# Four of six gated products of a chunk to ScalarE and GpSimd instead of three, with new order tables

## The reference

```
x = x + 0.5 * ffn(ln(x))
x = x + attn(ln(x))        # a selective scan (state space) block
x = x + 0.5 * ffn(ln(x))

ffn(v):  h = silu(v @ wg.T / 127) * (v @ wu.T / 127)      # 768 hidden channels
         return h @ wd.T / 127
attn(v): u  = silu(causal convolution of v with 4 taps)
         dt = softplus(v @ Wp[:64].T @ W_dt.T + b_dt)
         for each of 16 states s:  A~ = exp(dt * A_s),  B~ = (A~ - 1) / A_s
                                   h_s[t] = A~[t-1] * h_s[t-1] + B~[t-1] * u[t-1]
         y  = sum over s of C_s * h_s
         return ((y + u * D) * silu(v @ W_z.T)) @ W_out.T
```

## Time and profile before

| | |
|---|---|
| three runs | 2330.20, 2331.53, 2331.81 us (median 2331.53) |
| the profiled execution | 2330.55 us, of which the span is 2328.8 us |
| busy | PE 2129.7 us (91%), DVE 2169.8 (93%), ACT 1977.5 (85%), POOL 1817.2 (78%) |
| table loads on ScalarE | 271 in the loop and 1 ahead of it |
| first scan of row 0 starts | 88.42 us |
| first scan of row 1, row 14, row 15 starts | 236.26, 2017.50, 2150.78 us |
| last scan ends | 2278.05 us |
| granted TensorE clock | 0.977 over the span |

### The profile page before, as it was taken

How to read it: one execution, slowest core, us unless ns; L and a number is a source line. 1 busy time by engine, 2 the same in 40 slices (tenths; PEclk the granted TensorE clock), 3 DMA queues, 4 the chain that set the end, 5 groups by cost and what they waited for, 6 DMA issues and landing times. The chain is left out here.

```text
span 2328.8 us, 27774 instructions
## 1 busy us (share of the span) xinstructions
PE 2129.7 (91%) x8708; PEld 1280.0 (55%) x8708; DVE 2169.8 (93%) x2361; ACT 1977.5 (85%) x2876; POOL 1817.2 (78%) x1382
## 2 busy tenths in 40 slices
PE   7986999999999999999999999999999999999578
PEld 3452556556565555656555564655556465555246
DVE  2499999999999999999999999999999999999993
ACT  5988898898989889898988989888898988988772
POOL 2477788888888888888888888888887888888663
PEclk9997999999999999999999999999999999999779
DMA  2122344434344443443344334434434344333221
GB/s 89 38 74 72 131 139 138 143 128 150 133 141 140 137 143 131 140 142 145 136 137 143 129 136 143 148 136 137 145 128 145 137 137 145 137 127 124 73 66 38
DMA packets 112024, 291.15 MB, mean 125 GB/s; under 512 B 11201, under 2 KB 45314, under 8 KB 111874
## 3 DMA queue, kind: packets, MB, share of 16 engines
q1 hardware_dynamic: 111874, 289.35, 36.4%
HBM read 271.49 MB, written 17.83 MB: 124 GB/s over the span
## 5 line engine op out<-in xcount | busy, mean ns | idle before, releaser
L1118 POOL TENSOR_TENSOR acc<-acc,ring 128x1024 f32<-128x1024 f32 x512 | 1022.8, 1998 | 141.6 <-DVE ring L1314 131.0
L1278 DVE TENSOR_TENSOR_SCAN g_bank<-du_bank,ring 128x1024 f32<-128x1024 f32 (+1 forms) x512 | 1097.7, 2149 | 9.1 <-ACT du_bank L1021 6.6
L791 PE MATMUL work<-wd_t,hid 128*128 128x256 f32 x3072 | 681.5, 381 | 6.0 <-DVE hid L1231 5.1
L1314 DVE SCALAR_TENSOR_TENSOR ring<-g_bank,inv_a,ring 128x1024 f32<-128x1024 f32 (+1 forms) x576 | 662.3, 1155 | 9.9 <-POOL acc L1118 1.8
L791 PEld LDWEIGHTS work<-wd_t,hid 128*128 128x128 f32 x3072 | 584.1, 191 | 107.0 <-issue 14.8
L1039 ACT ACTIVATE ring<-dt,a_coef 128x1024 f32<-128x1024 f32 (+1 forms) x576 | 575.0, 1046 | 9.0 <-DVE g_bank L1278 7.9
L858 ACT ACT_TABLE_LOAD x271 | 347.7, 1283 | 4.9
L922 ACT ACTIVATE odd<-work 128x512 f32<-128x512 f32 x384 | 223.4, 601 | 110.5 <-PE work L779 108.0
L779 PE MATMUL work<-xt_hi,wg_t 128*128 128x512 f16 x768 | 296.0, 385 | 22.7 <-ACT odd L922 7.6
L779 PE MATMUL work<-xt_hi,wu_t 128*128 128x512 f16 x768 | 296.6, 386 | 20.1 <-ACT odd L922 14.4
L779 PE MATMUL work<-xt_lo,wu_t 128*128 128x512 f16 x768 | 296.0, 385 | 0.0
(11 more groups left out here) (98 smaller groups left out, 2635.2 us busy)
## 6 DMA issues: line engine op xcount, KB each, us to landing
ring<-c_rows SPq DMA_DIRECT2D x448, 512.0 KB, 3.6
ring<-c_rows SPq DMA_DIRECT2D x64, 256.0 KB, 3.2
x_in<-L_attn_x SPq DMA_DIRECT2D x30, 512.0 KB, 3.9
out<-x_fin SPq DMA_DIRECT2D x30, 512.0 KB, 4.8
x_fin<-L_attn_x SPq DMA_DIRECT2D x2, 512.0 KB, 5.9
c_rows<-params SPq DMA_DIRECT2D x32, 32.0 KB, 3.6
out<-x_in SPq DMA_DIRECT2D x2, 512.0 KB, 2.9
ring<-L_ffn_w_gate SPq DMA_DIRECT2D x1, 768.0 KB, 5.8
```

The source lines that it names most:

```text
L791: last = pe.matmul(dst[:, j * E:(j + 1) * E], hid[:, K.unit[f, bt, c, m] % HIDS, t:t + P], wd_t[:, m, :], start=(m == 0), stop=(m == HM - 1))
L1118: nc.gpsimd.tensor_tensor(v, v, shaped(bt, cg[:, K.number[ev[1:]] % TERMS, :]), ALU.add).then_inc(S["summed"], 1)
L1278: scan = nc.vector.tensor_tensor_scan(g, du_h, d_h, first[0], ALU.add, ALU.mult)
L1314: nc.vector.scalar_tensor_tensor(v, g, inv_a[:, h, s:s + 1], c_row, ALU.mult, ALU.mult).then_inc(S["weighted"], 1)
```

## The change

m = 1 joins 0, 2 and 4 in both feed-forward blocks: one of the three VectorE products of a chunk goes, and in its place ScalarE does one more copy out of PSUM and GpSimd one more product. That is 64 of each over the kernel: 16 rows, two blocks, two chunks. The five tables have new numbers throughout. `dn` now waits for the last of its `sh` and `hp` by their place in the list and not by the highest m, and `dt0` for whichever of its sums comes last. Nothing else is changed: same matmuls, tiles, buffers and transfers.

```diff
-POOLED = (0, 2, 4)
-OWN = (1, 3, 5)
+POOLED = {1: (0, 1, 2, 4), 2: (0, 1, 2, 4)}
+OWN = {f: tuple(m for m in range(HM) if m not in POOLED[f]) for f in POOLED}
...
 ROW = {
...
-    "sc1": [-35.454, -30.319, -27.9, -25.339, -22.957, -22.372],
-    "hp1": [-33.45, -29.15, -28.37, -23.334, -22.643, -22.332],
-    "sh1": [-32.255, -29.294, -26.295, -24.381, -20.683, -19.854],
-    "dn1": [-22.766, -22.537, -15.874, -15.226],
...
+    "sc1": [-34.21, -31.112, -28.501, -27.83, -25.852, -25.568, -22.962, -21.819],
+    "hp1": [-32.165, -31.402, -27.26, -27.88, -24.016, -24.475, -23.029, -20.86],
+    "sh1": [-27.982, -24.382, -20.207, -19.555],
+    "dn1": [-23.614, -23.248, -16.334, -15.399],
...
                 elif kind == "dn":
                     _, f, bt, c, jp = ev
                     hold(pe, s_cast, 3)
-                    wait(pe, "free", ("up", f, bt, c, OWN[-1]))
-                    wait(pe, "product", ("hp", f, bt, c, POOLED[-1]))
+                    wait(pe, "free", ("up", f, bt, c, max(OWN[f], key=lambda m: K.unit[f, bt, c, m])))
+                    wait(pe, "product", max((("hp", f, bt, c, m) for m in POOLED[f]), key=lambda job: K.at["product", job][1]))
...
-                        if was[-1] in POOLED:
+                        if was[-1] in POOLED[was[0]]:
...
-                    wait(act, "sp_sum", ("dp", bt, EH - 1, 0 if paired(bt) else NC - 1))
+                    made = [("dp", bt, h, c) for h in range(EH) for c in range(1 if paired(bt) else NC)]
+                    wait(act, "sp_sum", max(made, key=lambda job: K.at["sp_sum", job][1]))
```

More of the change, by code:

```diff
@@ L78 @@
 ROW = {
[60 rows of a table removed]
[L139 to L150, removed]
-        23.527, 27.535, 28.905],
@@ L152 @@
-    "op": [36.271, 36.973, 37.729, 39.665],
-    "rc": [35.662, 35.837, 37.781, 38.165],
-    "ra": [33.396, 34.218, 36.898, 42.906],
[60 rows of a table added]
+    "gate": [19.958, 32.034],
+    "scan": [0.213, 1.117, 2.593, 4.358, 5.349, 7.197, 7.625, 8.34, 9.445, 10.358, 11.389, 11.995, 13.207, 13.906,
+        15.384, 15.903, 16.687, 18.32, 19.159, 19.899, 20.145, 20.943, 21.856, 22.753, 23.339, 24.496, 25.654, 26.37,
+        27.576, 28.502, 29.719, 31.321],
+    "cm": [0.763, 2.558, 3.307, 4.92, 5.936, 7.602, 7.645, 9.259, 9.973, 11.247, 11.68, 12.76, 13.675, 14.855, 15.701,
+        16.238, 17.889, 19.05, 19.701, 20.074, 20.454, 21.836, 22.241, 23.055, 23.983, 24.827, 25.814, 27.11, 27.713,
+        28.928, 30.427, 31.538],
@@ new lines @@
+    "ln1": [-303.675, -256.114],
+    "lr1": [-82.654, -74.808],
+    "lx1": [-110.564, -87.071],
+    "T1": [-101.523, -53.378],
+    "Te1": [-97.902, -50.238],
+    "Ts1": [-99.169, -48.261],
+    "Tl1": [-91.93, -49.539],
+    "sj2": [-37.854, -34.885, -32.659, -31.835, -12.415, -12.329, -4.407, -4.043],
+    "ln2": [-24.792, -2.856],
+    "lr2": [-21.669, -4.775],
+    "lx2": [-21.063, 1.607],
+    "T2": [-15.367, 4.54],
+    "Te2": [-20.05, 2.156],
+    "ga1": [-82.598, -69.485, -56.827, -53.465, -52.215, -34.173, -35.219, -29.252, -28.985, -22.303, -21.242,
+        -16.595],
@@ new lines @@
+    "rs1": [-39.951, -32.814, -9.391, -6.512],
+    "rp": [-30.838, -26.409, -6.566, -5.941],
+    "pm": [-12.485, 7.115],
+    "pe": [-18.341, 5.51],
+    "cw": [-15.146, 6.451],
+    "cv": [-3.427, 10.227, -6.509, 13.772],
+    "us": [-13.875, 7.428, -13.766, 9.964],
+    "z": [4.728, 8.094, 15.273, 15.723],
+    "zs": [3.28, 5.4, 10.249, 14.709],
+    "dt": [-10.318, 10.19, -2.737, 15.485],
+    "da": [-16.899, 6.405, -12.887, 11.631],
+    "dl": [-14.958, 9.24, -11.602, 12.717],
+    "dp": [-10.273, 9.633, -9.525, 12.01],
@@ new lines @@
+    "rm": [0.73, 16.404, -0.749, 18.186],
+    "ai": [0.111, 12.635, -10.309, 16.146],
+    "aj": [0.623, 13.391, -7.852, 18.484],
+    "u0": [-11.158],
+    "dt0": [-8.994],
+    "d": [-8.345, 11.96],
+    "db": [-6.135, 13.086],
+    "gate": [14.708, 31.922],
+    "scan": [-3.781, 0.11, 1.556, 2.829, 3.481, 4.451, 5.102, 5.805, 6.741, 7.694, 8.338, 8.954, 9.864, 10.183,
+        12.705, 13.767, 14.812, 16.319, 18.496, 19.822, 20.516, 20.961, 22.117, 22.793, 23.175, 24.454, 24.679,
+        25.637, 28.915, 29.55, 31.209, 31.699],
@@ L254 @@
-    "aj": [-6.48, -0.135, -3.521, 0.441],
-    "u0": [-7.89],
-    "dt0": [-0.569],
+    "sj1": [-79.978, -62.758, -52.762, -49.836, -55.407, -53.356, -49.104, -46.604],
+    "ln1": [-47.654, -46.528],
+    "lr1": [-46.148, -42.123],
+    "lx1": [-48.763, -42.442],
+    "T1": [-34.812, -28.82],
+    "Te1": [-43.305, -32.122],
+    "Ts1": [-32.516, -28.741],
+    "Tl1": [-38.099, -31.771],
+    "sj2": [-24.449, -24.15, -21.832, -21.243, -17.672, -17.249, -13.901, -13.675],
+    "ln2": [-18.016, -13.348],
@@ new lines @@
+    "sc1": [-36.598, -35.608, -33.825, -28.326, -26.873, -25.732, -23.957, -22.76],
+    "hp1": [-35.708, -34.053, -34.548, -27.696, -24.35, -22.956, -24.072, -21.249],
+    "sh1": [-28.59, -27.633, -22.456, -20.86],
+    "dn1": [-23.87, -18.733, -14.264, -13.918],
+    "rs1": [-25.889, -23.937, -19.166, -18.038],
+    "rp": [-26.352, -22.731, -19.447, -18.484],
+    "pm": [-10.917, -10.372],
+    "pe": [-11.696, -11.149],
+    "cw": [-12.141, -1.516],
+    "cv": [-4.868, -5.739, -4.728, -6.625],
@@ L257 @@
+    "us": [-8.004, -8.846, -6.664, -6.542],
+    "z": [1.515, 5.426, 5.879, 13.725],
+    "zs": [-1.007, 4.337, 5.547, 11.264],
+    "dt": [-6.237, -6.058, -1.385, -4.164],
+    "da": [-11.111, -10.953, -3.604, -6.002],
+    "dl": [-5.549, -9.873, -2.707, -4.263],
+    "dp": [-5.386, -9.003, -2.63, -4.436],
+    "rm": [-2.629, -1.527, -3.197, -0.48],
+    "ai": [-5.778, -5.883, -6.449, -3.278],
+    "aj": [-2.577, -5.595, 1.0, -2.635],
+    "u0": [-6.096],
+    "dt0": [-1.571],
 }
 LATE = {
[20 rows of a table removed]
[20 rows of a table added]
 }
@@ L315 @@
-    "op": [23.261, 24.154, 44.889, 46.589],
-    "rc": [22.0, 22.363, 39.816, 46.194],
-    "ra": [21.844, 22.705, 45.325, 56.154],
[19 rows of a table added]
+    "gate": [15.254, 44.043],
+    "scan": [-0.319, 0.278, 0.623, 1.403, 2.382, 3.653, 5.734, 6.239, 7.481, 9.201, 9.722, 10.891, 11.786, 12.922,
+        14.222, 14.507, 15.214, 15.567, 16.279, 18.584, 20.236, 21.371, 22.376, 24.181, 25.341, 27.461, 29.689,
+        32.064, 34.041, 35.127, 36.83, 39.326],
+    "cm": [0.046, 0.341, 1.024, 2.216, 3.535, 4.049, 6.122, 6.517, 9.127, 9.428, 9.734, 11.688, 11.861, 14.035,
+        14.356, 14.75, 15.378, 16.029, 16.594, 19.232, 20.722, 21.489, 23.99, 24.481, 25.879, 27.605, 29.795, 32.467,
+        34.403, 35.527, 37.652, 40.723],
@@ L318 @@
+    "op": [20.494, 24.225, 53.337, 54.333],
+    "rc": [16.63, 19.283, 45.948, 48.68],
+    "ra": [15.756, 20.623, 56.439, 56.856],
 }
@@ L346, in row_events @@
             for m in range(HM):
-                for kind in ("ga", "si", "up") + (("sc", "hp") if m in POOLED else ("sh",)):
+                for kind in ("ga", "si", "up") + (("sc", "hp") if m in POOLED[f] else ("sh",)):
                     yield f"{kind}{f}", (kind, f, b, c, m)
```

109 lines of the change are left out of this document (43 added, 66 removed), and 231 rows, old and new, of tables (HEAD, LATE, ROW, TAIL).

## The result

The changed kernel takes 2249.6 us (median of four runs, 2247.59 to 2251.51) against 2331.0 (2330.2 to 2331.8) for the kernel before: a ratio of 0.9651, with a 95% interval of 0.9634 to 0.9667. The profiled execution took 2249.76 us, of which the span is 2248.0.

A forecast was written before the change was run, and what follows sets the result against it. VectorE's queue was taken to set the row, TensorE next. Savings of 34.2 (thirteen rows) + 4 (head) + 4 (row 0) + 2.0 (row 14) + 1.2 (row 15) = 45.4 us gave a median of 2286 us, range 2264 to 2320.

The forecast's parts named there:

- I keep these at 2.9: In a steady row, VectorE's waits stay at 2.9 us, so the row goes from 137.02 to 134.4 us.
- VectorE's work: In a steady row, four products fewer and two bare pairs fewer take 2.63 us off VectorE, leaving 131.5 us.
- Free, hidden beside VectorE: In a steady row, ScalarE's four more copies and two fewer table loads leave its work at about 121 us, costing nothing.
- Rival A: Steady rows: ScalarE releases TensorE's banks sooner, VectorE's waits fall to 1.2 us, row 132.7, total 2264 us; chance 0.13.
- Rival B: Steady rows: TensorE takes over, VectorE's wait grows to 5.5 us, row stays 137.0, total 2320 us; chance 0.19.
- Rival C: Steady rows: `dn` waits for GpSimd's products, row 141.9 us, total 2384 us, slower than before; chance 0.08.
- Rival D: Steady rows: through the shared SBUF port each GpSimd product stops VectorE, +1.7 us a row, total 2343 us; chance 0.04.
- Head: Up to the first scan: an earlier copy of x_mid and `rm` right after `dn` save 4 us, between 0 and 5.4.
- Row 0: First row: three VectorE products, six bare pairs and seven table loads fewer, -4 us, bounds +2 and -9.
- Row 14: Second-last row: three VectorE products and two bare pairs fewer save 2.0 us.
- Row 15: Last row: two VectorE products fewer ahead of its last `cm` save 1.2 us.
- After the last scan: Final stretch, where TensorE works through what is left: change of 0 us, bounds -4 and +5.

## Why the prediction was right and wrong

- **The step that failed** is "I keep these at 2.9", VectorE's waits in a steady row. They are 0.85. The reason given was double. First, "one us of them can't go": it was 0.51 us a row, at the row's first scan (the window of row 8 began and ended with this wait, so that the list counted it twice; it is not a wait at two halves, and the listed waits are 2.4 us and not 2.9), and in the new order it went whole. Second, that "the rest comes from TensorE, whose idle time would shrink from 6.6 to 3.9". Idle time of TensorE was a result of the chain and no supply of its own: it went to 1.7. The waits in the earlier trace rows were read as a fixed toll on VectorE; they were the ends of a chain of 137.07 us that a new list may shorten or lengthen. The row is 2.2 us below the forecast, 2.05 of it waits; in 13 rows that is 28.7 of the 35 us missed, and 26.7 by the waits.
- **VectorE's work** was right: 2.63 forecast, 2.79 measured, with 0.59 us for a product and 2.33 for a bare pair found again.
- **ScalarE** was right as to its sum (121 forecast, 120.33) and wrong in what it was taken for. "Free, hidden beside VectorE" can't be read from busy time: two loads cost 0, 1.43, 1.92, or 2.58 us and more, by place. Of their price, a load and the start of the next function are 1.30 us in the earlier trace rows, and the runs bear that out where the chain passes (2.58 for two). The Trainium skill (ScalarE: Activation LUTs, section What ACT_TABLE_LOAD costs) gives about 2.66 us for one switch; no row here shows that much.
- **Rival A** comes nearest: "waits shrink as well", a row of 132.7, 2264 us. It had 0.13. The measured 2249.6 us lie below it too: it was off by 0.5 in the row, in the head, in row 0 and in row 15. Its reason, fewer loads and so banks released sooner, is part of the cause: a pair of loads on the chain gave 1.43 us, one beside it nothing.
- **Rival B** fell for this order, but "TensorE takes the row over" is near to what the old order does with the same move: rows of 140, with `dn` waiting.
- **Rival C** is seen in the old order in another form: `dn` waits 2.8 us for the bank that ScalarE's copy frees and not for GpSimd. In the new one `dn` waits for no product of GpSimd's in the steady rows, as forecast.
- **Rival D** fell: the scans last 2260 to 2299 ns with GpSimd busy 89% of the time, as they did with 83%. The warning of the Trainium skill quoted there (Perfetto Trace Analysis, section Optimizing Scalar/DVE Operations) is not borne out for this pair of operations: the measurement decides.
- **The ends.** Head: right in kind, -7.5 against -4; what was missed is that the stretch ahead of the second `dn` also became shorter, by 2.6. Row 0: -9.9 against -4, outside the bound of -9; ten loads out of the old one gave 4.1. Row 14 about right. Row 15 had the wrong sign: I counted two VectorE products less and did not ask what stands in GpSimd's queue behind a product that waits for its copy. After the last scan: -1.3 against 0, within its bounds.

## What to carry to other kernels

When every engine runs a fixed list, the busiest engine's waits are not a toll that stays: find what they are the ends of, by walking from each wait to its releaser and on through that engine's queue, before you keep them in a sum. Here short waits that came back in every row, up to 1.0 us each, were ends of a chain round all engines, though ScalarE and GpSimd were idle 16 and 24 us in a row. Then work moved between engines counts by where it stands in the queues as much as by its length: the same move gave -81 us with one list and +52 with another. And before a saving is called nothing, compare rows at the same granted clock. The cost of an operation on an engine with slack must be bounded from zero to its whole length and more (0 to 4.3 us for two loads of 1.28 us here).
